# A decoder layer: staircase rows and ScalarE's high maxima in self-attention; sums of four heads and weighings once a pair in cross-attention

## The chip, the cores and the metric

The kernel runs on one core of a Trainium2 chip. The metric is the device time of one execution in microseconds, and the comparison goes by medians of several runs. Engines are named TensorE (PE), VectorE (DVE), ScalarE (ACT), GpSimd (POOL) and SyncE (SP, which only issues transfers here). PEld is TensorE's loading of weights.

## The reference

One layer of a pre-norm decoder on `x` (4 x 512 tokens, width 512), cut to what matters:

```
x = x + attn(layernorm(x))             # 32 query heads of 16, 8 key/value groups, causal, softmax
x = x + xattn(layernorm(x), ctx, ctx)  # per batch 8 heads of 64 rows, softmax over ctx's 512 columns
x = x + ffn(layernorm(x))              # ternary weights, 8-bit activations, gate and up 512->2048, down

def attn(x):   scores = q k^T / 4, masked where key > query; softmax(scores) v, then Wo
def xattn(q, k, v):                    # the tensors are split in heads along their rows (tokens)
    qk = einsum('bdm,bdn->bmn', qh, kh) / 8
    return einsum('bmn,bcn->bcm', softmax(qk, -1), vh)
```

## The kernel before

Each engine has its own program; semaphores tie them together. Three stretches follow each other.

**Self-attention.** `project_qkv` normalises and projects, with queries and keys split in three bf16 parts that are stacked in rows (`STACK` = 96 rows of `qs` and `ks`). There is one step for each pair of batch and group, 32 in all, software-pipelined: in step i TensorE computes the *first scores* of group i (`first_scores`, units F(0) to F(9), queries on the partitions), of which VectorE takes the maxima (`keep_maxima`, L148) with the causal mask `mask_qk` added; the maxima are transposed (`turn_maxima`, L137) and split in a high and a low bf16 row (`split_maxima`, L162 and L164), which `load_maxima` puts in rows 96 and 97 of `qs`. Two steps later the *second scores* S(0) to S(10) (keys on the partitions) contract 98 rows, so that the maximum is already subtracted (L852). The four of them that hold a diagonal block, S(0), S(5), S(8) and S(10), get a second matmul that adds the causal mask: `identb` against `mask_kq`, 4 heads x 128 columns (L855). ScalarE takes the exponential (L787), and `weigh` multiplies by the values in four 32-column tiles side by side (L870). ScalarE copies the result (L797), TensorE turns it (L836, slot `OUT`), VectorE divides (L806, L809). First scores, `OUT` and `TURN` share four banks in the order 0, 1, OUT, 2, TURN, 3 ... 9: a unit may start when the one four places earlier has been read. TensorE's order in a step is F0 S0 F1 S1 turn_outputs F2 S2 turn_maxima F3 S3 F4 S4, the weighings, then F5 S5 ... F9 S9 S10. SyncE and GpSimd load and quantise the feed-forward weights beside it.

**Output projection and cross-attention.** `rest_of_layer` projects, adds and normalises (`attend_output`), then runs `attend_context(i)`, one step for each head; two heads make a pair p. In step i TensorE runs the first scores of head i-1 (L1605, four matmuls over three banks; a matmul waits until the maximum three uses back has been taken) and the second scores of head i-4 (`second_scores`, L1633): four blocks, each the sum of four terms, of which the last subtracts the maxima from `mrows`. The terms run two blocks at a time. `weigh(p, 0)` and `weigh(p, 1)` follow in the odd step 2p+5, `weigh(p, 2)` and `weigh(p, 3)` in the even step 2p+6, all into the bank `pn` (L1646). VectorE takes four maxima a step (L1416), and in even steps the second total (L1446), the low keys (L1428) and the transposed maxima (L1422, `mt`), in odd steps the product with the inverse sums (L1465, `y_done`). GpSimd adds the probabilities (L1175, L1180) and adds the product to the tokens (L1184). ScalarE takes four exponentials a step (L1277), keeps weighted values (`keep_weighted`, L1256) and sums (`keep_sums`, L1305), and rounds keys (`keys`, L1246).

The way of the softmax sums: `sum_probs(p)` (L1661, in step 2p+8) multiplies the totals of the pair's two heads with ones, into two halves of a bank; ScalarE copies it (`den`), its queue moves two rows of it into `few` (step 2p+9), VectorE inverts (L1453, step 2p+10), SyncE writes the result to memory (step 2p+11, L1097) and spreads it over 64 rows for each head (step 2p+12, L1105, one buffer `rden`, behind a wait for the product of the pair before), VectorE multiplies (step 2p+13).

SyncE's program of an odd step begins with `load_maxima`: it waits for `mt_done` and issues four transfers `mrows` <- `mt` (L1044), which the last term of the first second scores in the next, even step waits for. Context rows, low queries and values follow. The queue is in order.

**Feed-forward.** `feed(i)` for 16 tiles of tokens; the last eight steps of `attend_context` run beside its first bodies.

Of the kernel before, what the change touches and what calls it, by code (L numbers as in the profile page):

```python
# [13 lines left out]
P = 128  # L14
# [61 lines left out]
class Steps:  # L76
# [9 lines left out]
    RING, RAW = 5, 6  # L86

# [66 lines left out]
def split_maxima(nc, dve, st, keep, i):  # L154
# [4 lines left out]
    dve.wait_ge(keep["p1_full"], st.use[i, st.TURN] + 1)  # L159
    if due(32 * (j // st.RING)):  # L160
        dve.wait_ge(keep["m_in"][j % st.RING], 32 * (j // st.RING))
    nc.vector.tensor_scalar(mrow[:, j % st.RING, 0, :], maxima, -1.0, None, ALU.mult).then_inc(keep["m_high"], 1)  # L162
# [33 lines left out]
def place_attention(nc, ctx, keep, st):  # L196
# [20 lines left out]
    over("vts", [P, SEQ], at["wg"] + 43 * KB)  # L217
    W = DIM + 2 * P
# [51 lines left out]
def project_qkv(nc, ctx, io, scr, keep, st):  # L270
# [39 lines left out]
    wo_high, padded = m.sem("wo_high"), m.sem("padded")  # L310
# [14 lines left out]
    def sync(sp):  # L325
# [10 lines left out]
        def load_x(b):  # L336
            sp.wait_ge(normed, TPB * b)
            sp.dma_start(x[:], x_d[b]).then_inc(x_in, 16)

# [11 lines left out]
        for b in range(BATCH):  # L351
# [17 lines left out]
            if b == 1:  # L369
                load_stacks(sp, st, scr, keep, 1)  # L370
            elif b == 2:
# [7 lines left out]
    def gpsimd(pool):  # L379
# [7 lines left out]
        for name in ("ident", "identb"):  # L387
# [7 lines left out]
                                base=0, pattern=[[0, GSZ], [1, P]], channel_multiplier=-1).then_inc(consts, 1)  # L395
# [29 lines left out]
        nc.gpsimd.memset(keep["ks"][STACK:P, :, :], 1.0).then_inc(padded, 1)  # L425
        pool.wait_ge(padded, 2)
        for b in range(BATCH):
# [10 lines left out]
    def scalar(act):  # L438
# [43 lines left out]
        for b in range(BATCH):  # L482
# [5 lines left out]
            high_part(b, 2)  # L488
            if more:
                high(b + 1, 0)  # L490
                high(b + 1, 1)
# [9 lines left out]
    def vector(dve):  # L501
# [33 lines left out]
        def early(b, idx):  # L535
            for i, k in early_after(b, idx):
                if k == st.TURN:
                    split_maxima(nc, dve, st, keep, i)
# [155 lines left out]
def self_attention(nc, ctx, io, scr, keep, st):  # L694
# [45 lines left out]
    def gpsimd(pool):  # L740
# [30 lines left out]
        pool.wait_ge(keep["last_out"], 16)  # L771
        pool.wait_ge(keep["scaled"], 3)
# [3 lines left out]
    def scalar(act):  # L776
        for i in range(LAST):
# [13 lines left out]
            for n in range(5):  # L791
                exponential(n)
            if 0 <= j3 < STEPS:
# [7 lines left out]
    def vector(dve):  # L801
# [11 lines left out]
        for i in range(st.EARLY_STEPS, LAST):  # L813
            for k in st.order:
# [4 lines left out]
                elif k == TURN:  # L819
                    split_maxima(nc, dve, st, keep, i)  # L820
# [3 lines left out]
    def tensor(pe):  # L824
        pe.wait_ge(keep["lo_done"], TILES)
        pe.wait_ge(keep["scaled"], 1)
        pe.wait_ge(keep["padded"], 2)
        for i in range(st.EARLY_STEPS, LAST):
# [10 lines left out]
            def second_scores(n):  # L839
# [51 lines left out]
def rest_of_layer(nc, io, scr, keep, out):  # L891
# [5 lines left out]
    PAIRS = HEADS_X // 2  # L897
# [947 lines left out]
```

## Time and profile before

| | |
|---|---|
| median of 3 runs | 792.17 us (792.15 to 793.11) |
| the profiled execution | 791.34 us, its span 789.5 us |
| TensorE busy | 758.5 us, 96% of the span |
| VectorE busy | 637.8 us, 81% |
| ScalarE busy | 491.1 us, 62% |
| GpSimd busy | 423.1 us, 54% |
| self-attention steps | about 93 to 373 us |
| output projection | about 373 to 435 us |
| cross-attention steps | about 435 to 597 us |
| feed-forward | to the end |

Matmuls overlap in the profile: one of 512 columns lasts 0.38 us and the next starts 0.22 us after it, so starts are read, not durations. A matmul in fp32 is recorded as two. Busy time says little of who waits; the bracket at the end of a timeline row does: the engine's idle time ahead of the row and who ended it. The granted clock is 1.00 (2.4 GHz) nearly everywhere.

### The profile page before, as it was taken

To read this page: it belongs to the slowest core of one execution; us is meant where nothing else is said; L and a number is where in the kernel's file an instruction comes from. 1 tells how busy PE (TensorE), PEld (TensorE's weight loads), DVE (VectorE), ACT (ScalarE), POOL (GpSimd) and SP (SyncE) were. 2 spreads that over 40 slices of the span, in tenths; PEclk is the share of its full clock that TensorE was granted. 3 is DMA by queue.
4 is the path that set the end of the run, shared out by engine and by line. 5 is a ranking of instruction groups with operands and counts; after the bars stand their busy time and mean duration, and the time that the engine had idled before them with its cause. 6 is when DMAs were issued, how large, how long until landed. Compare 5 with 4: busy or idle time off the path is not lost.

```text
span 789.5 us, 15365 instructions
## 1 busy us (share of the span) xinstructions
PE 758.5 (96%) x4832; PEld 420.6 (53%) x4886; DVE 637.8 (81%) x1905; ACT 491.1 (62%) x844; POOL 423.1 (54%) x459
## 2 busy tenths in 40 slices
PE   8999999999999999998999899999998999999998
PEld 6777544444444444443777555555543455455543
DVE  7676888889888889881589878888977899888883
ACT  4665567667766776676355555555556576567564
POOL 5554489999999700000234367777886444423331
PEclk9999999999999999999899999999999999999999
DMA  8898674444544311200486434444420011000001
GB/s 289 301 385 282 210 186 136 122 132 133 139 128 130 96 54 52 61 18 3 146 284 236 162 108 136 134 136 135 121 70 18 11 42 41 28 15 27 28 26 42
DMA packets 65888, 94.79 MB, mean 120 GB/s; under 512 B 27184, under 2 KB 38576, under 8 KB 64272
## 3 DMA queue, kind: packets, MB, share of 16 engines
q1 hardware_dynamic: 61344, 80.77, 32.5%
q0 software_dynamic: 3952, 12.98, 5.8%
q8 instruction: 39, 0.64, 0.3%
q14 instruction: 41, 0.34, 0.1%
q10 hardware_dynamic: 512, 0.07, 0.1%
HBM read 72.88 MB, written 20.51 MB: 118 GB/s over the span
## 4 chain that ended last, share of the span: by engine, by line
PE 40%; DVE 5%; issue 3%; ACT 2%; POOL 1%; SPq 0%; DMA 0%; ACTq 0%; DVEq 0%; POOLq 0%
PE r_p L1698 12%; PE r_p L1633 7%; PE r_pn L1646 7%; PE r_p L1728 3%; PE r_pn L1728 3%; PE r_p L1605 3%; PE r_p L1661 2%; PE r_p L1712 2%; DVE r_stats L1384 1%; DVE tok L1403 1%; PE r_p L1587 1%; DVE r_xl L1397 1%; ACT r_xn L1235 1%; DVE r_mx L1416 0%; DVE r_h L1500 0%
## 5 line engine op out<-in xcount | busy, mean ns | idle before, releaser
L787 ACT ACTIVATE b_probs<-ab_j 128x512 f32<-128x512 f32 (+1 forms) x352 | 176.7, 560 | 25.5 <-PE ab_j L852 14.6
L148 DVE CUSTOM_DVE_ANT_0 b_junk<-ab_t,mask_qk 128x128 bf16<-128x128 f32 (+2 forms) x243 | 108.7, 485 | 27.0 <-PE ab_t L128 26.7
L852 PE MATMUL ab_j<-qs,ks 98*128 98x512 bf16 (+1 forms) x352 | 121.8, 361 | 2.9 <-DMA qs<-mrow 1.1
L1277 ACT ACTIVATE r_probs<-r_p 128x512 f32<-128x512 f32 x128 | 69.5, 599 | 65.2 <-PE r_p L1633 63.8
L148 DVE CUSTOM_DVE_ANT_0 b_junk<-ab_e,mask_qk 128x256 bf16<-128x256 f32 (+2 forms) x237 | 103.6, 482 | 0.3 <-issue 0.2
L1416 DVE TENSOR_REDUCE r_mx<-r_p 128x1 f32<-128x512 f32 x128 | 82.4, 675 | 22.1 <-PE r_p L1605 21.2
L1175 POOL TENSOR_TENSOR r_halves<-r_probs 128x1024 f32<-128x1024 f32 x32 | 76.6, 2395 | 34.8 <-DVE r_total L1446 24.9
L1327 ACT ACTIVATE r_silu<-r_p,r_cg 128x512 f32<-128x512 f32 x64 | 44.2, 691 | 53.0 <-PE r_p L1698 51.7
L870 PE MATMUL ab_pv<-b_probs,v 128*32 128x512 f32 (+3 forms) x1024 | 75.6, 436 | 0.0
L1202 POOL TENSOR_SCALAR r_h<-r_h,r_fh 128x1024 f32<-128x1024 f32 x32 | 38.0, 1199 | 64.8 <-DVE r_fh L1546 64.8
L128 PE MATMUL ab_e<-ks,qs 96*128 96x128 bf16 (+3 forms) x269 | 64.0, 300 | 5.3 <-DVE mx L148 0.7
L1698 PE MATMUL r_p<-wu,r_zt 128*128 128x512 bf16 x251 | 65.4, 379 | 0.3
L1698 PE MATMUL r_p<-wg,r_zt 128*128 128x512 bf16 x245 | 63.5, 379 | 2.1 <-ACT r_zt L1367 1.4
L1646 PE MATMUL r_pn<-r_probs,r_vt 128*64 128x512 f32 x256 | 61.3, 599 | 0.5 <-ACT r_y L1256 0.5
L128 PE MATMUL ab_t<-ks,qs 96*128 96x128 bf16 (+2 forms) x243 | 58.6, 301 | 2.4 <-DVE mx L148 0.2
L1500 DVE TENSOR_TENSOR r_h<-r_p,r_silu 128x512 f32<-128x512 f32 x64 | 44.0, 687 | 18.7 <-PE r_p L1698 10.7
L870 PEld LDWEIGHTS ab_pv<-b_probs,v 128*32 128x32 f32 x1024 | 30.0, 109 | 48.3 <-issue 41.6
L1130 POOL MEMSET r_mrows<- 128x1024 f32 x1 | 1.0, 952 | 101.7 <-POOLq L238 101.7
L797 ACT ACTIVATE b_osb<-ab_pv 128x512 f32<-128x512 f32 x32 | 19.1, 597 | 58.2 <-PE ab_pv L870 58.2
L852 PEld LDWEIGHTS ab_j<-qs,ks 98*128 98x128 bf16 x352 | 34.1, 97 | 26.5 <-ACT b_probs L787 10.4
L1508 DVE TENSOR_REDUCE r_hpart<-r_h 128x1 f32<-128x512 f32 x64 | 43.9, 686 | 2.2
L128 PEld LDWEIGHTS ab_e<-ks,qs 96*128 96x128 bf16 x269 | 22.9, 98 | 39.6 <-DVE mx L148 14.8
(177 smaller groups left out, 1761.3 us busy)
## 6 DMA issues: line engine op xcount, KB each, us to landing
qs<-q_parts SPq DMA_DIRECT2D x32, 192.0 KB, 3.3
q_parts<-a_parts SPq DMA_DIRECT2D x15, 384.0 KB, 6.1
a_wst<-in_w_gate SPq DMA_DIRECT2D x4, 1024.0 KB, 7.7
a_wst<-in_w_up SPq DMA_DIRECT2D x4, 1024.0 KB, 9.9
a_wst<-in_w_down SPq DMA_DIRECT2D x4, 1024.0 KB, 8.3
qs<-q_parts SPq DMA_DIRECT2D x32, 128.0 KB, 3.2
b_wst<-in_w_gate POOLq DMA_DIRECT2D x16, 256.0 KB, 3.8
b_wst<-in_w_up POOLq DMA_DIRECT2D x16, 256.0 KB, 3.3
```

The source lines that it names most:

```text
L128: last = nc.tensor.matmul(st.bank(keep, i, k)[:, c:c + w], keep["qs"][0:STACK, s, j, qt * P:(qt + 1) * P], keep["ks"][0:STACK, s, 0:w], st ...
L148: best = nc.vector.tensor_tensor_reduce(out=junk[:, 2 * (st.use[i, k] % slots) + n, 0:w], in0=bank[:, c:c + w], in1=keep["mask_qk"][:, SEQ ...
L787: nc.scalar.activation(pblock(j % 2, kb)[:, j0:j0 + nj, c:c + w], p2[(NE * j + n) % BANKS2][:, 0:nj * w].rearrange("p (j c) -> p j c", j=n ...
L852: last = nc.tensor.matmul(bank, ks[0:STACK + 2, s, kb * P:(kb + 1) * P], qs[0:STACK + 2, s, j0:j0 + nj, kb * P + c:kb * P + c + w], start= ...
L870: last = nc.tensor.matmul(pv[2 * HDIM * j:2 * HDIM * (j + 1), kb * P:], v, pblock(j3 % 2, kb)[:, j, :], start=kb == 0, stop=kb == TPB - 1, ...
L1175: nc.gpsimd.tensor_tensor(halves[:], probs[:, slot, 0:2, :], probs[:, slot, 2:4, :], ALU.add).then_inc(halved, 1)
L1277: nc.scalar.activation(probs[:, 2 * (p % 2) + a, blk, :], p2_bank("s", j, n)[:], ACT.Exp, scale=SCALE).then_inc(p2_used, 1)
L1416: nc.vector.reduce_max(mx[:, p % 2, KD * a + blk:KD * a + blk + 1], p1_bank("f", i, n)[:], AX.X).then_inc(p1_used, 1)
L1633: last = nc.tensor.matmul(p2_bank("s", j, 2 * b + a)[:], weights, right[rows, :], start=term == 0, stop=term == 3)
L1646: last = nc.tensor.matmul(pn[a * H:(a + 1) * H, :], vt[:, 2 * (p % 2) + a, nb, :], probs[:, 2 * (p % 2) + a, nb, :], start=nb == 0, stop=n ...
L1698: last = nc.tensor.matmul(bank[g % len(bank)][:], zt[:, j % 2, k, :], keep[w][:, k, n * 512:(n + 1) * 512], start=k == 0, stop=k == KD - 1)
L1728: last = nc.tensor.matmul(pf[j % 2][:], ht[j % 2][:, k, :], keep["wd"][:, k, :], start=k == 0, stop=k == KF - 1)
```

## The change

In self-attention:

- The causal mask of the diagonal blocks is put partly into the stacks. Rows 98 to 127 (30 = `STAIRS`) of `ks` get -1e30 where row and key agree, and those rows of `qs` are one for the queries from 97 up to the one before that row. The diagonal second scores contract 128 rows instead of 98, and the mask matmul covers 97 (`FLAT`) of a head's 128 columns. GpSimd makes the pattern (two fills, three selections), and SyncE copies it to all slots (`load_stairs`, 30 rows x 100 copies of 256 bytes) behind the stacks of step 1.
- The high maxima are taken by ScalarE (`maxima_high`), after its third exponential of the step, and VectorE, which takes the low ones, waits for that.

In cross-attention:

- `sum_probs` sums four heads at once, in four 32-column tiles, every second even step (10, 14, ...). The copy, the move into `few`, the inverse and the transfers are once for four heads too; the inverse and its way to memory are in steps 13 + 4q, SyncE's spreading in steps 14 + 4q (two buffers `rden`, each behind a wait for the product that last read it).
- The product and the addition to the tokens move from step 2p+13 to 2p+17, with six buffers `y` and eight for the totals.
- The four `weigh` of a pair all run in the even step 2p+6.
- `attend_context` has four more steps, beside feed-forward bodies.

The diff, cut to what sets order and waits:

```diff
+    STAIRS = P - STACK - 2
+    FLAT = P - STAIRS - 1
...
+def maxima_high(nc, act, st, keep, i):
+
+    j = i - 1
+    act.wait_ge(keep["p1_full"], st.use[i, st.TURN] + 1)
+    if due(32 * (j // st.RING)):
+        act.wait_ge(keep["m_in"][j % st.RING], 32 * (j // st.RING))
+    nc.scalar.activation(keep["mrow"][:, j % st.RING, 0, :], st.bank(keep, i, st.TURN)[0:st.BLOCKS, 0:P], ACT.Copy,
+                         scale=-1.0).then_inc(keep["m_high"], 1)
...
+        def load_stairs():
+
+            sp.wait_ge(stairs_done, 3)
+            rows = slice(P - st.STAIRS, P)
+            for part, name, copies in ((0, "ks", st.RING * TPB), (1, "qs", st.RING * GSZ * TPB)):
...
             for n in range(5):
                 exponential(n)
+                if n == 2 and i >= st.EARLY_STEPS and (i, TURN) in st.use:
+                    maxima_high(nc, act, st, keep, i)
...
-                last = nc.tensor.matmul(bank, ks[0:STACK + 2, s, kb * P:(kb + 1) * P],
-                                        qs[0:STACK + 2, s, j0:j0 + nj, kb * P + c:kb * P + c + w], start=True, stop=c > 0)
+                rows = slice(0, P) if c == 0 else slice(0, STACK + 2)
+                last = nc.tensor.matmul(bank, ks[rows, s, kb * P:(kb + 1) * P],
+                                        qs[rows, s, j0:j0 + nj, kb * P + c:kb * P + c + w], start=True, stop=c > 0)
                 if c == 0:
-                    last = nc.tensor.matmul(bank, keep["identb"][:], keep["mask_kq"][:].rearrange("p j c -> p (j c)"), start=False, stop=True)
+                    last = nc.tensor.matmul(bank.rearrange("p (j c) -> p j c", j=GSZ)[:, :, 0:st.FLAT], keep["identb"][:], keep["mask_kq"][:],
+                                            start=False, stop=True)
...
-                p = pair_due(i, 11)
-                if p is not None:
-                    sp.wait_ge(inv_done, p + 1)
...
-                p = pair_due(i, 12)
-                if p is not None:
-                    sp.wait_ge(inv_out, 16 * (p + 1))
-                    if due(p):
-                        sp.wait_ge(y_done, p)
...
+                q = quad_due(i, 13)
+                if q is not None:
+                    sp.wait_ge(inv_done, q + 1)
...
+                q = quad_due(i, 14)
+                if q is not None:
+                    sp.wait_ge(inv_out, 16 * (q + 1))
+                    for p in (2 * q, 2 * q + 1):
+                        if due(p - 1):
+                            sp.wait_ge(y_done, p - 1)
+                        for a in range(2):
+                            at = RUNS * (2 * p + a)
+                            sp.dma_start(rden[a * H:(a + 1) * H, p % 2, :], scr["inv"][at:at + RUNS, :].rearrange("r c -> (r c)")
+                                         .unsqueeze(0).broadcast_to([H, DIM])).then_inc(rden_in[p % 2], 16)
...
-                p = pair_due(i, 13)
+                p = pair_due(i, 17)
                 if p is not None:
-                    dve.wait_ge(rden_in, 32 * (p + 1))
+                    dve.wait_ge(rden_in[p % 2], 32 * (p // 2 + 1))
                     dve.wait_ge(y_kept, p + 1)
...
-                p = pair_due(i, 8)
-                if p is not None and p < LATE_SUMS:
-                    sum_probs(p)
-                p = pair_due(i, 5)
-                if p is not None:
-                    weigh(p, 0)
-                    weigh(p, 1)
+                q = quad_due(i, 10)
+                if q is not None and q < QUADS - 1:
+                    sum_probs(q)
                 p = pair_due(i, 6)
                 if p is not None:
-                    weigh(p, 2)
-                    weigh(p, 3)
-                if i == 2 * LATE_SUMS + 8:
-                    sum_probs(LATE_SUMS)
+                    for nb in range(KD):
+                        weigh(p, nb)
```

## Rows read from the trace of the kernel before

**Rows 1.** Timeline, VectorE, one self-attention step: start, us, engine, line, operation, [idle before]

```profile
203.21 0.29 DVE L148 CUSTOM_DVE_ANT_0 b_junk<-ab_t,mask_qk 128x128 bf16<-128x128 f32 x1 [0.93 <-PE ab_t L128]
...
208.10 0.42 DVE L809 TENSOR_TENSOR tok<-ab_t,b_rec 128x256 f32<-128x256 f32 x1
...
209.13 0.27 DVE L162 TENSOR_SCALAR mrow<-ab_e 16x128 bf16<-16x128 f32 x1
...
211.94 0.29 DVE L148 CUSTOM_DVE_ANT_0 b_junk<-ab_t,mask_qk 128x128 bf16<-128x128 f32 x1 [0.93 <-PE ab_t L128]
```

**Rows 2.** Timeline, TensorE, the same step

```profile
204.61 0.38 PE L855 MATMUL ab_j<-mask_kq,identb 128*128 128x512 bf16 x1
...
204.83 0.38 PE L128 MATMUL ab_t<-ks,qs 96*128 96x512 bf16 x1
...
208.59 0.39 PE L128 MATMUL ab_t<-ks,qs 96*128 96x512 bf16 x1
...
209.07 2.36 PE L870 MATMUL ab_pv<-b_probs,v 128*32 128x512 f32 x32
...
211.36 0.39 PE L128 MATMUL ab_t<-ks,qs 96*128 96x128 bf16 x2
```

**Rows 3.** Timeline, ScalarE, the same step

```profile
208.55 1.12 ACT L787 ACTIVATE b_probs<-ab_j 128x384 f32<-128x384 f32 x2 [0.29 <-PE ab_j L852]
```

**Rows 4.** Timelines; window table (from:to, length, engines busy, PEclk, DMA share, GB/s)

```profile
19.20 0.24 POOL L401 TENSOR_SCALAR a_veps<-a_mv 128x4 f32<-128x4 f32 x1 [2.14 <-DVE a_mv L511]
...
64.00:65.00 1.00, 1.00 (x6) 0.75 (x4) 1.00 (x3) 0.00 (x0) 0.96 (x1) 1.00 0.09 32
...
85.33 1.65 DVE L586 TENSOR_SCALAR wo_hi<-a_wraw 128x2048 fp32r<-128x2048 f32 x1 [1.52 <-DMA a_wraw<-in_wo]
```

**Rows 5.** Window table, cross-attention steps 17 to 32

```profile
500.38:579.79 79.41, 79.12 (x482) 42.47 (x480) 68.81 (x109) 45.55 (x87) 62.80 (x37) 1.00 0.44 125
```

**Rows 6.** Timeline, TensorE, cross-attention: end of step 12, step 13

```profile
477.93 1.08 PE L1661 MATMUL r_p<-r_total,ones 128*64 128x512 f32 x4
...
478.83 1.89 PE L1646 MATMUL r_pn<-r_probs,r_vt 128*64 128x512 f32 x8
...
480.65 0.49 PE L1605 MATMUL r_p<-r_kh,r_qh 64*128 64x512 f32 x2
...
481.91 0.52 PE L1605 MATMUL r_p<-r_kh,r_qh 64*128 64x512 f32 x2
...
483.29 1.94 PE L1646 MATMUL r_pn<-r_probs,r_vt 128*64 128x512 f32 x8
...
485.15 0.50 PE L1605 MATMUL r_p<-r_kh,r_qh 64*128 64x512 f32 x2
```

**Rows 7.** Timeline, VectorE, the same steps

```profile
477.65 0.53 DVE L1453 RECIPROCAL r_inv<-r_few 16x64 f32<-16x64 f32 x1
...
481.18 2.49 DVE L1416 TENSOR_REDUCE r_mx<-r_p 128x1 f32<-128x512 f32 x4
...
483.58 0.78 DVE L1465 TENSOR_TENSOR r_y<-r_y,r_rden 128x512 f32<-128x512 f32 x1
```

**Rows 8.** Timeline, ScalarE, the same steps

```profile
482.60 0.59 ACT L1256 ACTIVATE r_y<-r_pn 128x512 f32<-128x512 f32 x1
```

**Rows 9.** Timelines: SyncE in steps 12 and 13; the first maxima and their matmul

```profile
479.06 1.14 SPq L1105 DMA_DIRECT2D r_rden<-inverse_sums  x2
...
481.07 2.21 SPq L1044 DMA_DIRECT2D r_mrows<-r_mt  x4
...
435.69 2.35 SPq L1044 DMA_DIRECT2D r_mrows<-r_mt  x4
...
439.08 0.78 PE L1633 MATMUL r_p<-r_mrows,r_unit 64*128 64x512 f32 x2 [0.40 <-DMA r_mrows<-r_mt]
```

**Rows 10.** Timeline, TensorE; window table behind its idle time

```profile
436.29 0.49 PE L1605 MATMUL r_p<-r_kh,r_qh 64*128 64x512 f32 x1 [2.06 <-DVE r_mx L1416]
...
437.00:446.00 9.00, 8.56 (x46) 6.01 (x48) 8.01 (x14) 6.32 (x11) 0.18 (x2) 0.81 0.57 183
```

More of the change, by code:

```diff
@@ L488, in scalar @@
             high_part(b, 2)
+            if (1, st.TURN) in early_after(b, 2):
+                maxima_high(nc, act, st, keep, 1)
             if more:
@@ L1011, in p2_bank @@
         def p2_bank(*key):
-            return p2[SBANKS - 1] if key[0] == "sum" and key[1] >= LATE_SUMS else p2[p2_use[key] % SBANKS]
+            return p2[SBANKS - 1] if key == ("sum", QUADS - 1) else p2[p2_use[key] % SBANKS]
         def pair_due(i, behind):
@@ L1017, in pair_due, with quad_due @@
             return s // 2 if s >= 0 and s % 2 == 0 and s < HEADS_X else None
+        def quad_due(i, behind):
+            s = i - behind
+            return s // 4 if s >= 0 and s % 4 == 0 and s < HEADS_X else None
         @block.sync
@@ L1282, in attend_context @@
                     keep_weighted(p)
-                p = pair_due(i, 9)
-                if p is not None:
-                    act.wait_ge(p2_used, p2_use["sum", p] + 1)
-                    if due(p - 1):
-                        act.wait_ge(inv_done, p - 1)
-                    for a in range(2):
-                        act.dma_start(few[a * RUNS:(a + 1) * RUNS, p % 2, :],
-                                      den[a * H:a * H + 1, :].rearrange("o (r c) -> o r c", r=RUNS)).then_inc(few_in, 16)
+                q = quad_due(i, 11)
+                if q is not None:
+                    act.wait_ge(p2_used, p2_use["sum", q] + 1)
+                    if due(q - 1):
+                        act.wait_ge(inv_done, q - 1)
+                    act.dma_start(few[:, q % 2, :], den[0:3 * PART + 1:PART, :].rearrange("a (r c) -> a r c", r=RUNS)).then_inc(few_in, 16)
                 exponential(1)
@@ L1649, in weigh, with sum_probs @@
                     last.then_inc(weighted, 1)
-            def sum_probs(p):
-                pe.wait_ge(first_total, p + 1)
-                pe.wait_ge(second_total, p + 1)
-                if p < LATE_SUMS:
-                    pe.wait_ge(p2_used, p2_use["sum", p] - SBANKS + 1)
-                elif p == LATE_SUMS:
+            def sum_probs(q):
+                pe.wait_ge(first_total, 2 * q + 2)
+                pe.wait_ge(second_total, 2 * q + 2)
+                if q < QUADS - 1:
+                    pe.wait_ge(p2_used, p2_use["sum", q] - SBANKS + 1)
+                else:
                     pe.wait_ge(p2_used, P2_USES)
-                else:
-                    pe.wait_ge(p2_used, p2_use["sum", p - 1] + 1)
-                for a in range(2):
-                    last = nc.tensor.matmul(p2_bank("sum", p)[a * H:(a + 1) * H, :], keep["ones64"][:], total[:, 2 * (p % 2) + a, :], start=True, stop=True)
+                for a in range(4):
+                    last = nc.tensor.matmul(p2_bank("sum", q)[a * PART:(a + 1) * PART, :], keep["ones64"][:, 0:PART], total[:, (4 * q + a) % TSLOTS, :],
+                                            start=True, stop=True)
                 last.then_inc(summed, 1)
```

131 lines of the change are left out of this document (72 added, 59 removed).

## The prediction

> **What bounds the kernel now.** I read three views in this order: the busy table by windows, to see in which stretch TensorE leaves time; then the timelines of TensorE and VectorE side by side through one self-attention step and through one pair of cross-attention steps; last SyncE's issues in that pair, because the change moves waits on that queue. The reader should see two different limits.
>
> In self-attention TensorE looks busy almost throughout, but it does not set the pace. VectorE starts a step's first reduction after the weighing at 203.21 and again at 211.94: a step of 8.73 us [rows 1]. In between it runs without a pause until `tok` is written at 208.52 (208.10 + 0.42). Only then is the bank of `OUT` free for unit 4: TensorE starts it at 208.59, and from there go unit 4, S(4), the weighings (`x32`, from 209.07), unit 5 at 211.36, and VectorE's 211.94 [rows 1, 2]. This loop sets the step: 5.31 us of VectorE, then 3.35 us of TensorE in which no mask matmul lies, plus 0.07 us between.
>
> In cross-attention TensorE is the limit: eight pairs of steps (17 to 32) take 79.41 us with 79.12 us busy [rows 5]. An odd step lasts 4.50 us (480.65 to 485.15): scores until the weighing starts at +2.64, then 1.86 us for half of the weighings. An even step adds the sum, 0.90 us (477.93 to 478.83) [rows 6]. I count times below from the start of an odd step, "+".
>
> **Self-attention: nothing.** The mask matmul takes 0.22 us from start to start (204.61 to 204.83) for 512 columns; 388 columns save 0.053 us, and 128 of them 6.8 us [rows 2]. All four of a step (S(0), S(5), S(8), S(10)) lie between unit 5 and unit 3 of the next step, beside VectorE's unbroken 5.31 us. With that cover they are worth 0; without it -6.8, which I keep as the bound. The staircase rows widen a contraction from 98 to 128 rows and add no column; the mask matmul itself already contracts 128 rows at 0.22 us, so 0. VectorE gives up the high maxima, 0.27 us, at 209.13, in the part of the step that ends in 0.93 us of waiting [rows 1]: 0, while it waits longer. ScalarE takes them after its third exponential, where it has 0.29 us idle and the next exponential starts at 208.55 [rows 3]; the shortest thing near it is VectorE's 0.27, the longest its own 0.60 us for 512 columns [rows 8]. Either ends before VectorE asks at 209.13, so the new wait of VectorE (behind it are the low maxima and unit 3) costs 0. GpSimd's five new operations lie in its 2.14 us of idle time ahead of 19.20 us; the fill there is paid. The two staircase transfers (3,000 pieces, 0.77 MB) enter SyncE's queue behind the stacks of step 1, some microseconds ahead of the stretch 64 to 65 us. In that stretch the DMA engines have 91% of their time free, so most of that queue is worked off; what is left could delay `wo`, on which VectorE already waited 1.52 us at 85.33 [rows 4]. I count 0.4 us for that and 0.3 us gained because VectorE, which is the limit just before the steady steps, has one operation less: 0, between -7 and +1.5.
>
> **Cross-attention, work of TensorE.** A sum of four costs what a sum of two did if the four 32-column tiles run together. The self-attention weighing does that: 32 matmuls of 320 columns on average in 2.29 us (209.07 to 211.36) [rows 2], against 8 of 512 columns in 1.86 us for 64-column tiles [rows 6], twice the rate. So 0.90 us per quad; one after another it would be 1.8. The weighings of a pair are together 3.72 us, and an odd step without them runs into the next with +2.41 (two halves of 1.26, 480.65 to 481.91, less the 0.11 for the change of tile shape that the first half holds and the second does not). TensorE alone would then need 2.41 + 2.64 + 3.72 = 8.77 us a pair and 0.45 for its half of a sum, 9.2 instead of 9.9.
>
> **What stops it: the queues beside it.** With three score banks, the last first-score matmul of a step waits for the first maximum of the same step. In an odd step VectorE runs four maxima from +0.53 to +3.02 and then the product, 2.93 to 3.71 [rows 7]. The next step's first maximum ends some 0.65 later, and the matmul can start at +4.36 instead of +3.67: before, the weighing of the odd step covered that. Before step 17 there is no product; then ScalarE decides, which keeps the weighted values at +1.95 (0.59 us) and so ends its second exponential at about +3.05 [rows 8]; the four terms that wait for its bank take 0.95, and that matmul starts at +4.05. After it come 1.38 us of scores and 3.72 of weighings. The reciprocal, now in odd steps, puts 0.5 us (0.53 long [rows 7]) ahead of the product in every second pair, and that pair is also the one with the sum: 4.36 + 0.5 + 1.38 + 0.90 + 3.72 = 10.86 us.
>
> The other pairs have a worse wait. SyncE issues in order. At step 14 + 4q it now spreads the inverse sums of pairs 2q and 2q + 1, and for the second it waits for `y_done` of product 2q - 1. That product (`pair_due(i, 17)` on VectorE) runs in step 15 + 4q, the step after. Queued behind the wait is everything SyncE issues for that step: first the four transfers of the maxima (`load_maxima`) which S(0) of step 16 + 4q needs for its last term. Today they are issued right behind VectorE's transpose, at 481.07, +0.42. With the change SyncE wakes at +3.71 and issues two broadcasts, 1.14 us, to +4.85. The time from the first of the four issues to the matmul that waited for it is seen once: 435.69 to 439.08, 3.39 us [rows 9]. So this matmul starts at about +8.3 instead of +3.8: TensorE stands 4.5 us. The pair then takes 8.27 + 0.23 + 1.38 + 3.72 = 13.6 us. Four pairs have it: q = 1 to 4, steps 19, 23, 27, 31 (for q = 0 there is no wait, for q = 5 no maxima are left). The context rows behind it, needed by ScalarE's `keys` in the same even step, land at about +10.1; the low keys and the transpose end near +13, before the next step: no more.
>
> The clock comes on top. After TensorE's idle 2.06 us before 436.29 the stretch 437 to 446 shows a granted clock of 0.81, that is 3.4 us at 1.2 instead of 2.4 GHz, costing 1.7 us of matmul time [rows 10]. Here it stands twice as long; I take 1.7 for each of the four, bounds 0 and 3.4. The Trainium skill, "TensorE: Matmul & The Clock Gate", section "HAM oscillation — how this bites in real kernels", says that a loop which waits for a transfer between groups of matmuls falls to half clock every time and pays anew; the trace has one case, which agrees. By that rule the time is the one below, without it 6.8 us less, the second rival.
>
> **The sum.** Pairs of steps 17 to 32: 4 x (10.86 + 13.6 + 1.7) = 104.6, against 79.4: +25.2. Pairs of steps 5 to 16: 8.8 (steps 5, 6), three of 4.05 + 1.38 + 3.72 = 9.15 and two of 10.1 with the sum make 56.4, against 9.0 + 5 x 9.9 = 58.5: -2.1. Steps 33 to 36 lose about 0.9 to ScalarE (no weighing beside the exponentials), and the feed-forward part starts one sum, 0.9, earlier: 0. The later products (two more beside the feed-forward steps) lie on VectorE where it is not the limit. Together +23. The profiled execution took 791.34 us (span 789.5), 0.8 below the median 792.17; 791.3 + 23.1 = 814.4, on the median's scale 815.
>
> **Rivals.** First, TensorE's work decides everywhere: mask -6.8, early pairs 54.4 against 58.5 (-4.1), late pairs 8 x 9.22 = 73.8 against 79.4 (-5.6), so -16.5: 776, faster. For it speaks the full TensorE row; against it the 0.93 us of VectorE's loop and the order of the wait on `y_done`, which is in the diff. It decides if VectorE's chain were shorter than TensorE's 2.41 us step. Chance 0.08. Second, the stalls without the clock: +16.3, 808.5; the single case speaks against it, but it lay beside other short gaps. 0.17. Third, the wait of SyncE is harmless (maxima early enough): 4 x (10.86 + 9.46) = 81.3, +1.9 - 2.1, 792, within 0.2%; it needs a slack of a whole step that I don't see. 0.06. Fourth, four-column sums one after another or a second period at half clock: +6 to +7 on the forecast, 821. 0.09. The forecast itself: 0.60, own range 810 to 819.
>
> **Numbers.** 815 us. Leaving out the first and third rival and some of the spread: 802 to 823. Faster by over 0.2% (about what a measurement of this kernel can tell) 0.08, within 0.2% 0.05, slower 0.87.
>
> **What would show it.** Four gaps of 4 to 5 us on TensorE between third and fourth term of S(0), released by the `r_mrows` transfer; SyncE waiting for L1465's product at those four places; granted clock 0.5 behind them; other pairs at about 10.9 us; self-attention steps still 8.73 us, with shorter mask matmuls and longer waits for VectorE. A step of 8.5 us there, or no gap at steps 20, 24, 28 and 32, would make the prediction wrong.

## The result, and the profile after

The changed kernel takes 816.58 us (median of four runs, 814.09 to 819.54); the kernel before takes 792.16 us beside it. The ratio is 1.032, with a 95% interval of 1.030 to 1.035: slower, as forecast (815, range 802 to 823). The profiled execution took 814.09 us with a span of 812.4; that of before took 791.34 with 789.5. So 22.9 us of span are to be found.

First the page of the changed kernel: busy time by engine, then the group of the last score term (L1681 is what L1633 was: busy us, mean ns, idle us just before it and its releaser).

```profile
PE 758.9 (93%) x4886; PEld 420.2 (52%) x4886; DVE 632.4 (78%) x1865; ACT 487.4 (60%) x868; POOL 423.5 (52%) x464
...
L1681 PE MATMUL r_p<-r_mrows,r_unit 64*128 64x512 f32 x128 | 34.4, 435 | 18.0 <-DMA r_mrows<-r_mt 18.0
```

TensorE is busy for the same 758.9 us as before (758.5), although it has less to do (part of the work now runs at half clock, as shown below), and it stands 18.0 us waiting for the maxima's transfer. The kernel before stood 0.4 us there. The timeline of TensorE through the first long pair, steps 19 and 20 (start, us, engine, line, operation, idle before):

```profile
499.65 0.50 PE L1653 MATMUL r_p<-r_kh,r_qh 64*128 64x512 f32 x1 [0.30 <-DVE r_mx L1464]
...
501.02 1.06 PE L1707 MATMUL r_p<-r_total,ones 128*32 128x512 f32 x8
502.02 3.65 PE L1694 MATMUL r_pn<-r_probs,r_vt 128*64 128x512 f32 x16
505.60 0.50 PE L1653 MATMUL r_p<-r_kh,r_qh 64*128 64x512 f32 x2
...
509.03 0.62 PE L1681 MATMUL r_p<-r_ql,r_kh 64*128 64x512 f32 x2
513.95 0.80 PE L1681 MATMUL r_p<-r_mrows,r_unit 64*128 64x512 f32 x2 [4.30 <-DMA r_mrows<-r_mt]
514.54 0.63 PE L1653 MATMUL r_p<-r_kh,r_qh 64*128 64x512 f32 x2
...
516.81 5.29 PE L1694 MATMUL r_pn<-r_probs,r_vt 128*64 128x512 f32 x16
522.02 0.50 PE L1653 MATMUL r_p<-r_kh,r_qh 64*128 64x512 f32 x2
```

The odd step 19 starts at 505.60. The fourth term of S(0) of step 20 starts at 513.95, at +8.35, after 4.30 us of standing. Behind it the same matmuls take longer: the sixteen weighings 5.29 us instead of 3.65. The pair lasts 16.42 us. The same stretch by windows (from:to, length, busy of PE, PEld, DVE, ACT, POOL, then the granted clock, DMA share, GB/s):

```profile
512.00:513.00 1.00, 0.00 (x0) 0.00 (x0) 0.00 (x0) 0.00 (x0) 1.00 (x1) 1.00 0.09 32
513.00:514.00 1.00, 0.05 (x2) 0.06 (x2) 0.00 (x0) 0.00 (x0) 0.92 (x2) 0.66 0.01 2
514.00:516.00 2.00, 2.00 (x10) 1.62 (x12) 0.80 (x2) 1.14 (x3) 1.92 (x2) 0.50 0.89 293
...
520.00:521.00 1.00, 1.00 (x6) 0.28 (x4) 0.00 (x0) 0.00 (x0) 0.00 (x0) 0.93 0.01 1
```

The granted clock falls to 0.50 while TensorE still stands and is back at 1.00 at about 520.1: some 6.8 us at 1.2 GHz. Between 512 and 513 GpSimd alone works. What SyncE does in that time (its issues), and the product that it waits for:

```profile
501.47 9.12 SPq L1154 DMA_DIRECT2D r_rden<-inverse_sums  x4
510.69 2.22 SPq L1092 DMA_DIRECT2D r_mrows<-r_mt  x4
```
```profile
504.60 0.21 DVE L1470 STREAM_TRANSPOSE r_mt<-r_mx 128x32 f32<-128x32 f32 x1
506.14 2.48 DVE L1464 TENSOR_REDUCE r_mx<-r_p 128x1 f32<-128x512 f32 x4 [1.33 <-PE r_p L1653]
508.54 0.68 DVE L1513 TENSOR_TENSOR r_y<-r_y,r_rden 128x512 f32<-128x512 f32 x1
```

VectorE has turned the maxima at 504.8. SyncE issues their transfers at 510.69, because of the four broadcasts ahead of them: the first two are issued from 501.47, the other two wait for the product, which ends at 509.22. The transfers of the maxima, which [rows 9] show at +0.42 of the odd step, are now at +5.09.

The starts of the odd steps, read off TensorE's timelines of the kernels (the first L1653 behind the weighings; with split weighings two steps make a pair), give the length of each pair. All tables below are built so:

| pairs, us | steps 7 to 16 | steps 17 to 32 |
|---|---|---|
| before | 9.85, 9.86, 9.85, 9.86, 9.87 | 9.83 to 9.87, one of 10.5 |
| after | 8.93, 9.93, 9.13, 9.98, 8.93 | 10.61, 16.42, 10.60, 16.71, 10.59, 16.70, 10.60, 14.98 |

Steps 7 to 16 give 2.4 us back, steps 17 to 32 cost 107.2 instead of 79.4 us. The rest of the span, from the start to step 7, is 3.0 us shorter, and between step 33 and the feed-forward part 0.55 us are lost; together +22.9 (-3.0 - 2.4 + 27.8 + 0.5). The self-attention steps are 8.73 us as before.

### The profile page after: what moved, and what is told of

It is laid out like the page before. It is cut to its first block, busy times and chain, and to the rows that moved or that the text cites. A ratio compares the mean times of both kernels' runs of the same rounds, so it can differ in the third digit from the quotient of the medians.

```text
span 812.4 us, 15336 instructions
## 1 busy us (share of the span) xinstructions
PE 758.9 (93%) x4886; PEld 420.2 (52%) x4886; DVE 632.4 (78%) x1865; ACT 487.4 (60%) x868; POOL 423.5 (52%) x464
## 4 chain that ended last, share of the span: by engine, by line
PE 36%; DVE 8%; issue 3%; ACT 2%; SPq 2%; POOL 1%; DMA 1%; DVEq 0%; POOLq 0%; ACTq 0%
PE r_p L1739 12%; PE r_pn L1694 8%; PE r_p L1681 5%; PE r_p L1769 3%; PE r_pn L1769 3%; DVE r_mx L1464 3%; PE r_p L1753 2%; PE r_p L1653 2%; DVE r_stats L1432 1%; PE r_p L1707 1%; SPq L1092 1%; DVE tok L1451 1%; DMA r_mrows<-r_mt 1%; DVE r_xl L1445 1%; SPq L1154 1%
## 5 line engine op out<-in xcount | busy, mean ns | idle before, releaser
L824 ACT ACTIVATE b_probs<-ab_j 128x512 f32<-128x512 f32 (+1 forms) x352 | 172.7, 560 | 24.1 <-PE ab_j L893 15.2
L893 PE MATMUL ab_j<-qs,ks 128*128 128x512 bf16 (+2 forms) x352 | 121.9, 361 | 2.6 <-DMA qs<-mrow 1.4
L1739 PE MATMUL r_p<-wg,r_zt 128*128 128x512 bf16 x256 | 65.7, 379 | 1.4 <-ACT r_zt L1415 1.4
L1694 PE MATMUL r_pn<-r_probs,r_vt 128*64 128x512 f32 x256 | 63.4, 640 | 0.0
L1681 PE MATMUL r_p<-r_mrows,r_unit 64*128 64x512 f32 x128 | 34.4, 435 | 18.0 <-DMA r_mrows<-r_mt 18.0
L893 PEld LDWEIGHTS ab_j<-qs,ks 98*128 98x128 bf16 (+1 forms) x352 | 34.2, 97 | 23.2 <-ACT b_probs L824 12.2
```

The source lines that it names most:

```text
L824: nc.scalar.activation(pblock(j % 2, kb)[:, j0:j0 + nj, c:c + w], p2[(NE * j + n) % BANKS2][:, 0:nj * w].rearrange("p (j c) -> p j c", j=n ...
L893: last = nc.tensor.matmul(bank, ks[rows, s, kb * P:(kb + 1) * P], qs[rows, s, j0:j0 + nj, kb * P + c:kb * P + c + w], start=True, stop=c > 0)
L1681: last = nc.tensor.matmul(p2_bank("s", j, 2 * b + a)[:], weights, right[rows, :], start=term == 0, stop=term == 3)
L1694: last = nc.tensor.matmul(pn[a * H:(a + 1) * H, :], vt[:, 2 * (p % 2) + a, nb, :], probs[:, 2 * (p % 2) + a, nb, :], start=nb == 0, stop=n ...
L1739: last = nc.tensor.matmul(bank[g % len(bank)][:], zt[:, j % 2, k, :], keep[w][:, k, n * 512:(n + 1) * 512], start=k == 0, stop=k == KD - 1)
```

## The experiments

Each kernel was timed beside the kernel before on the same chip, and the ratio is to that. The median of before was 789.1 to 791.4 on those chips.

### The wait on SyncE

**spread_late.** The spreading of the second pair is moved to where its product is already done.

```diff
-                    for p in (2 * q, 2 * q + 1):
-                        if due(p - 1):
-                            sp.wait_ge(y_done, p - 1)
...
+                    spread(2 * q)
+                q = quad_due(i, 16)
+                if q is not None:
+                    spread(2 * q + 1)
```

> The changed kernel with one thing moved: SyncE spreads the inverse sums of pair 2q + 1 in step 16 + 4q instead of 14 + 4q, when the product that it waits for is already done. My theory: the four standstills of 4.5 us and the half clock behind them all vanish, and the gaps of TensorE ahead of the last term of S(0) in steps 20, 24, 28 and 32 with them. The four pairs take about 10 us instead of 16.4, 16.4, 16.7 and 15: 64.5 - 40 = 24.5 less than the changed kernel, so 792. Rival 1 (the transfer of the maxima itself, or its queue, is late whatever SyncE waits for): the gaps stay, 812 or more. Rival 2 (the half clock does not come from the standstill but from the longer chains of the odd steps): the gaps vanish, 0.5 of granted clock stays, about 805.

Measured: 791.39 us, ratio 1.001 (0.999 to 1.003). The waits for the maxima are gone and the clock is 1.00 in steps 17 to 32. SyncE's issues in the same place now:

```profile
503.47 1.14 SPq L1159 DMA_DIRECT2D r_rden<-inverse_sums  x2
506.64 2.23 SPq L1092 DMA_DIRECT2D r_mrows<-r_mt  x4
```

The pairs of steps 17 to 32 begin 10.59, 9.22, 10.60, 9.21: the pair that took 16.4 takes 9.22. The later four are 11.07, 10.12, 10.61 and some 9.2 us, with no wait of TensorE over 0.9 us. Both rivals fall; the one moved wait carries the whole loss. What is left of the change is worth nothing in sum.

**filled.** The wait stays, and TensorE gets something to do in it.

```diff
+                again = 6 if b == 0 and j in (16, 20, 24, 28) else 0
+                for at, (term, (left, right)) in enumerate(terms[0:3] * again + terms):
```

> The changed kernel with the first three terms of the first score group computed seven times instead of once in steps 20, 24, 28 and 32, where TensorE otherwise stands 4.5 us: 18 more pairs of matmuls of 0.23 us, 4.2 us, the last set is the one that counts. SyncE's wait stays. Theory (a pair with a stall costs 4.5 us of standing and about 3 us of half clock that the standing brings): the pairs of 16.4 to 16.7 us become about 13.7, granted clock 1.00 in them, and the median is some 10 us below the changed kernel's, 805 to 807. Rival 1 (the half clock has another cause): pairs and time as in the changed kernel, 814 to 819. Rival 2 (the transfer waits for something of TensorE's): the gap moves behind the fill and the time rises.

Measured: 805.25 us, ratio 1.020 (1.017 to 1.023). Windows over the first and the last of the four pairs with the wait, of the changed kernel and then of this one:

```profile
505.60:522.02 16.42, 12.09 (x58) 6.14 (x56) 9.13 (x12) 5.25 (x10) 9.21 (x5) 0.79 0.27 82
...
587.22:602.20 14.98, 10.43 (x58) 5.76 (x56) 10.68 (x16) 4.72 (x9) 9.97 (x6) 0.89 0.19 55
```
```profile
510.95:524.72 13.77, 13.29 (x96) 8.39 (x94) 9.50 (x12) 5.18 (x10) 9.34 (x5) 1.00 0.32 97
...
583.02:596.30 13.28, 12.67 (x92) 8.37 (x92) 9.38 (x13) 4.72 (x9) 9.35 (x5) 1.00 0.25 61
```

With matmuls in place of the standing the clock stays at 1.00. The four pairs take 53.55 us instead of 64.81: the half clock costs 11.3 us, 2.8 a pair. Against the 9.22 us of a pair without the wait the remaining 13.4 leave 4.2 for the wait itself. So of the 7.0 us that a wait costs, 4.2 are the queue and 2.8 the clock.

The 2.8 is a mean of unequal parts. In the changed kernel the fourth wait is as long as the others (4.50 us), but its low clock ends sooner:

```profile
595.00:596.00 1.00, 0.23 (x2) 0.23 (x4) 0.00 (x0) 0.00 (x0) 0.92 (x2) 0.62 0.05 5
...
598.00:599.00 1.00, 1.00 (x6) 0.20 (x4) 1.00 (x1) 0.27 (x1) 1.00 (x1) 0.68 0.04 9
```

That is 3.4 us at 1.2 GHz instead of 6.8, and the pair is 1.70 us longer than its filled counterpart (14.98 against 13.28), where the other three are 2.65 to 3.46 us longer. What decides between 3.4 and 6.8 no run shows.

### The order of the product and of the weighings

Both on top of spread_late.

**product_even.** The product goes back to even steps, one step later; the spreading follows it.

```diff
-                p = pair_due(i, 17)
+                p = pair_due(i, 18)
```

> The kernel of the late spreading, with the product and its addition moved back to the even steps (one step later than in the changed kernel), and the spreading with it. My theory: in the changed order the product delays the next step's first maximum, so odd steps without a weighing run into a stop ahead of their fourth score group; with the product in even steps the pairs with and without the sum lose about 0.3 to 0.6 us each over eight pairs: 3 us less than the late spreading, 789. Rival (ScalarE's exponentials limit there anyway, as in the early pairs): no difference, within 1 us.

Measured: 788.66 us, ratio 0.999 (0.997 to 1.002), 2.7 below spread_late, whose interval it overlaps. In the profiled executions the pairs are shorter: 10.00, 8.95, 9.99, 9.02 instead of 10.59, 9.22, 10.60, 9.21, and steps 17 to 30 take 68.0 instead of 71.4 us. As a whole that execution is not faster (790.93 against 790.09), because its first copy of weighted values in self-attention comes 4.6 us later, at 111.6 instead of 107.1 (the start of the kernel is treated below). So the gain is seen in the steps of one execution each and not shown in the time.

**weigh_split.** The sixteen weighings of a pair are split over two steps as before.

```diff
+                p = pair_due(i, 5)
+                if p is not None:
+                    weigh(p, 0)
+                    weigh(p, 1)
                 p = pair_due(i, 6)
                 if p is not None:
-                    for nb in range(KD):
-                        weigh(p, nb)
+                    weigh(p, 2)
+                    weigh(p, 3)
```

> The kernel of the late spreading, with the weighings of a pair in two groups in two steps as before, so that the change keeps the sum of four, the product in odd steps and the self-attention part. My theory: the half of the weighings in the odd step covers the wait for the bank of scores again and TensorE is busy throughout; the sum of four, 1.0 us per four heads instead of 0.9 per two, leaves a pair at about 9.45 instead of 9.9 us: 14 pairs, 6 us below the kernel before, 786. Rival (four-column sums save nothing, since the sum itself takes longer than two did or a wait takes its place): 791 to 792.

Measured: 787.33 us, ratio 0.997 (0.995 to 1.000). Pairs alternate between 10.58 and 8.99 us, 9.78 on average and not the 9.45 I worked out. The long one holds an odd step of 5.09 us (500.60 to 505.69) where others take 4.50. VectorE ahead of its maxima, and TensorE's row in that step:

```profile
499.05 1.96 DVE L1481 TENSOR_TENSOR r_kl<-r_k,r_kh 128x512 fp32r<-128x512 f32 x1
500.93 0.68 DVE L1469 TENSOR_REDUCE r_mx<-r_p 128x1 f32<-128x512 f32 x1
501.64 0.21 DVE L1475 STREAM_TRANSPOSE r_mt<-r_mx 128x32 f32<-128x32 f32 x1
501.78 1.25 DVE L1469 TENSOR_REDUCE r_mx<-r_p 128x1 f32<-128x512 f32 x2
```
```profile
502.48 0.50 PE L1658 MATMUL r_p<-r_kh,r_qh 64*128 64x512 f32 x1 [0.20 <-DVE r_mx L1469]
```

The low keys, 1.96 us, lie in the even step ahead. That step has no sum now in every second pair and is 1.0 us shorter, so the last maximum of it is reduced only at 500.93, 0.33 us into the odd step, and the odd step's first ends at 502.4, after TensorE has asked for its bank: the weighings begin 1.94 us after the third first score (501.88 to 503.82) where the next step has 1.34 (506.97 to 508.31). In the pair with the sum the same maximum starts 0.67 us ahead of the odd step (510.51 to 511.18) and nothing waits. The kernel before needs 19.7 us for two pairs, this one 19.57: a sum of four saves 0.7 us in the even steps, and the 0.59 of the odd step gives most of it back.

**split_even.** Both together, with the wide staircase pieces of a later section.

> All that the earlier runs point to, without the looser order in self-attention: late spreading, product in even steps, weighings split over two steps, staircase of wide pieces. With the product in even steps alone the pairs took 10.0 and 8.95 us; with the split alone 10.58 and 8.99, where the reciprocal and the product in one odd step cost 0.6. Theory: both together give 10.0 and 8.95 with a last sum started earlier (1.7 us less ahead of the feed-forward part), and the head as in the kernel before: some 6 us below it, 783.5 to 785. Rival (the split's gain and the even product's are the same gain): as the product in even steps with a good head, 786.

Measured: 797.72 us, ratio 1.009 (1.007 to 1.011). The expectation missed, on the far side of both theories, and the reason that it gives for the 0.6 us (reciprocal and product in one step) is not what the rows above show. From step 17 on, most steps come out at 5.07, 4.50, 6.06 and 5.49 us where weigh_split has 4.51, 4.49, 5.09 and 5.49. VectorE and TensorE at such a place:

```profile
519.30 0.93 DVE L1518 TENSOR_TENSOR r_y<-r_y,r_rden 128x512 f32<-128x512 f32 x1
520.15 1.28 DVE L1469 TENSOR_REDUCE r_mx<-r_p 128x1 f32<-128x512 f32 x2
```
```profile
520.88 0.50 PE L1658 MATMUL r_p<-r_kh,r_qh 64*128 64x512 f32 x1 [1.09 <-DVE r_mx L1469]
```

The product stands behind the transposition, ahead of the odd step's maxima, and pushes them by 0.85 us, on top of the late low keys. With whole weighings TensorE spends 3.6 us in front of that step and VectorE catches up; with the weighings split it has 1.9 us, and TensorE waits 1.09. The place of the product was tried in both places of the weighings, but split_even also has the wide staircase pieces, which lie ahead of these steps. In these rows the place of the product is good or bad only together with the place of the weighings.

### Self-attention

**self_only.** The kernel before with the self-attention part of the change alone.

```diff
+                rows = slice(0, P) if c == 0 else slice(0, STACK + 2)
-                    last = nc.tensor.matmul(bank, keep["identb"][:], keep["mask_kq"][:].rearrange("p j c -> p (j c)"), start=False, stop=True)
+                    last = nc.tensor.matmul(bank.rearrange("p (j c) -> p j c", j=GSZ)[:, :, 0:st.FLAT], keep["identb"][:], keep["mask_kq"][:],
+                                            start=False, stop=True)
```

> The kernel before with the self-attention part of the change alone: staircase rows, mask matmuls of 388 instead of 512 columns, high maxima on ScalarE. My theory: VectorE's loop sets the step, so it stays 8.73 us and the time stays within 1 us of before (791 to 793), with more idle time of TensorE ahead of unit 4 or longer waits. Rival (TensorE's time counts): 128 masks less 0.053 us each, steps of about 8.5 us, 785.5.

Measured: 794.38 us over twelve runs, ratio 1.003 (1.001 to 1.006): the steps are 8.73 us, as the theory has it, but the ratio puts the kernel 2.5 us above before (0.4 to 4.5), which it hasn't. The steps first. VectorE's and TensorE's rows of the changed kernel that answer to [rows 1, 2]:

```profile
212.01 0.29 DVE L150 CUSTOM_DVE_ANT_0 b_junk<-ab_t,mask_qk 128x128 bf16<-128x128 f32 x1 [1.25 <-PE ab_t L130]
```
```profile
208.02 0.39 PE L130 MATMUL ab_e<-ks,qs 96*128 96x128 bf16 x2 [0.25 <-DVE mx L150]
```

VectorE waits 1.25 us at the end of its loop instead of 0.93, which is the high maxima that it gave up; TensorE waits 0.25 us ahead of a unit where the timeline of before shows no wait (207.96), which fits the masks' saving of four times 0.053 us. The step stays.

**two_masks.** The mask of one unit a step issued twice, on the kernel before.

```diff
+                for turn in range(0 if c else 2 if n == 5 else 1):
```

> The kernel before with the mask matmul of one of the four masked units of each self-attention step (S(5)) issued twice: 32 matmuls of 0.22 us more, 7.0 us of TensorE's work. Theory (all masks lie beside VectorE's unbroken 5.31 us, so TensorE's time there counts for nothing as long as its slack of some 0.4 us a step lasts): steps stay 8.73 us, time within 1 us. Rival (TensorE's work counts in the step): steps of 8.95 us, 7 us more.

Measured: 794.90 us, ratio 1.005 (1.003 to 1.007), steps of 8.90 us. Neither theory had 0.17. The rows say why:

```profile
215.17 0.29 DVE L148 CUSTOM_DVE_ANT_0 b_junk<-ab_t,mask_qk 128x128 bf16<-128x128 f32 x1 [0.93 <-PE ab_t L128]
...
215.87 0.08 DVE L148 DVE_READ_ACCUMULATOR2_ANT mx<- 128x1 f32 x1
216.04 0.69 DVE L148 CUSTOM_DVE_ANT_0 b_junk<-ab_e,mask_qk 128x512 bf16<-128x512 f32 x1
```

VectorE's third reduction follows the first at +0.87 where the kernel before has +0.70 (203.21 to 203.91): S(5)'s mask lies ahead of the unit that this reduction needs, TensorE was only 0.05 us ahead of VectorE there (the reduction starts 0.57 us behind its matmul when it waits for it, at 215.47 and 216.04, and 0.62 us behind it in before, at 212.03 and 212.65), and 0.22 - 0.05 = 0.17 reach the step. So the loop stands, but it is tight: a mask taken away gives nothing, a mask added at this place costs three quarters of its time.

**loop_before, loop_self.** The looser order of a step, on the kernel before and on self_only. ScalarE copies the weighted values two exponentials later.

```diff
-            W(0); W(1); W(2); W(3)
-            F(5); S(5); F(6); S(6); F(7); S(7); F(8); S(8); F(9); S(9); S(10)
+            W(0)
+            F(5); S(5); W(1); F(6); S(6); W(2); W(3); F(7); S(7); F(8); S(8); F(9); S(9); S(10)
```

> The kernel before with the order of a self-attention step loosened: one of the four weighing groups stays ahead of unit 5, one follows S(5), two follow S(6), and ScalarE copies the weighted values two exponentials later. Masks are as before, 512 columns. Theory (the step is a loop of 5.31 us VectorE and 3.35 us TensorE, of which 2.29 us are weighings): the loop loses most of the weighings, and TensorE's own work, about 8.3 us, sets the step: 32 steps less 0.4 each, 778 to 780. Rival (TensorE's work sets the step of 8.73 already): no gain, 791.

> The same looser order on the kernel with the self-attention part of the change: masks of 388 columns, high maxima on ScalarE. Theory (the mask's 6.8 us were worth nothing only because VectorE's loop hid them): with TensorE at its limit they now count, 4 times 0.053 us a step, about 0.2 us a step and 6 us in all below the looser order on the kernel before, apart from what the staircase transfers cost ahead of the first step. Rival (the staircase saves nothing on TensorE): within 1 us of it, or above.

Measured: 797.43 us, ratio 1.010 (1.007 to 1.012), and 798.91 us, ratio 1.011 (1.008 to 1.013). Steps are 9.00 and 8.95 us. Both theories missed; only the rival for the second kernel, nothing gained on the first, is near. TensorE in one such step:

```profile
204.85 1.06 PE L872 MATMUL ab_pv<-b_probs,v 128*32 128x512 f32 x8
...
206.61 0.85 PE L872 MATMUL ab_pv<-b_probs,v 128*32 128x384 f32 x8
...
207.93 0.86 PE L872 MATMUL ab_pv<-b_probs,v 128*32 128x256 f32 x16
```

The weighings take 1.00 + 0.79 + 0.79 = 2.58 us in three places (start to start of what follows) instead of 2.29 in one, and VectorE waits 0.49 and 0.63 us for units behind them. TensorE is busy 8.78 us of the 9.00; it was 8.48 of 8.73. My 8.3 us for TensorE's own work was wrong: apart from gaps of 0.25 us it needed the step already. So TensorE's work fills the new step to within 0.22 us; how much of that rest is VectorE's was not measured. In the looser order the shorter masks are worth 0.05 us a step, not 0.2. Whether a looser order of another shape would let them count stays open.

### The start of the kernel

In the profiled run of self_only the copies of the weighted values begin at 112.2 us instead of 106.4. VectorE's row for `wo`, and SyncE's issues behind the staircase:

```profile
90.31 1.23 DVE L622 TENSOR_SCALAR wo_hi<-a_wraw 128x2048 fp32r<-128x2048 f32 x1 [4.67 <-DMA a_wraw<-in_wo]
```
```profile
58.12 1.06 SPq L355 DMA_DIRECT2D ks<-a_stairs  x1
59.24 0.90 SPq L355 DMA_DIRECT2D qs<-a_stairs  x1
60.25 6.28 SPq L364 DMA_DIRECT2D q_parts<-a_parts  x1
```

The wait for `wo` is 4.67 us instead of 1.52 [rows 4], and the issue right behind the staircase takes 6.28 us. In the window 90 to 100 us the granted clock is 0.66.

**stairs_early.** The same two transfers behind the stacks of step 0.

```diff
             if b == 0:
                 load_stacks(sp, st, scr, keep, 0)
+                load_stairs()
```

> The kernel with the self-attention part alone, with its two staircase transfers issued on SyncE behind the stacks of step 0 instead of step 1, some 22 us earlier. In the profiled run of the self-attention part alone the store behind the staircase transfers took 6.3 us to be issued and the load of wo was late: VectorE waited 4.7 us for it, and the first context copy of self-attention came at 112.2 instead of 106.4. Theory (the 3,000 small pieces of the staircase hold the queue, and wo behind them): here the wait for wo is back at about 1.5 us, the first context copy at about 106.5, and the median 3 us lower, at 790 to 791. Rival (the head of the kernel varies by itself, the staircase has no part): no difference to the self-attention part alone.

Measured: 790.12 us, ratio 1.001 (0.999 to 1.002); the wait for `wo` is 2.62 us (1.5 expected), the first copy at 108.4 (106.5 expected).

**wide_stairs.** A source of 512 columns, a quarter of the pieces.

```diff
-    over("stairs", [P, 2, P], at["wg"] + 45 * KB, BF16)
+    over("stairs", [P, 2, SEQ], at["wg"] + 45 * KB, BF16)
```

> The kernel with the self-attention part alone, with a staircase source of 512 instead of 128 columns, so that the two transfers consist of a quarter of the pieces (750 of 1 KB instead of 3,000 of 256 bytes) for the same 0.77 MB, at the same place in SyncE's queue. GpSimd's five operations on it are wider. Theory (the number of small pieces holds the queue ahead of wo): the store behind the staircase is issued in about 1.6 us instead of 6.3, VectorE waits about 1.5 us for wo, and the median is that of the kernel before, within 1 us. Rival (the bytes count, or GpSimd's operations): as the self-attention part alone, 3 to 4 us above the kernel before.

Measured: 791.15 us, ratio 1.000 (0.999 to 1.002).

```profile
86.75 2.08 DVE L622 TENSOR_SCALAR wo_hi<-a_wraw 128x2048 fp32r<-128x2048 f32 x1 [1.09 <-DMA a_wraw<-in_wo]
```
```profile
61.17 0.56 SPq L364 DMA_DIRECT2D q_parts<-a_parts  x1
61.84 2.98 SPq L364 DMA_DIRECT2D k_parts<-a_parts  x1
```

The issue behind the staircase takes 0.56 us, the one after it 2.98, and `wo` is waited for 1.09 us. Both kernels are level with before where self_only is not, so the small pieces explain its loss best. But the intervals touch (self_only from 1.001, stairs_early up to 1.002), and the wait for `wo` varies by itself. Of the seven profiled kernels with narrow pieces behind step 1, four waited 3.67 to 4.67 us and three 1.12 to 2.42, the changed kernel (1.43) and spread_late (1.12) among the latter although the issue behind the staircase took 6.07 and 5.56 us there. The kernels with wide pieces waited 0.62 to 2.56 us, stairs_early 2.62, and before, loop_before and two_masks, which have no staircase, 1.31 to 2.47. That the small pieces cause the long waits is likely and not shown.

**split_wide.** The best two parts together: weigh_split with wide pieces.

> The kernel with the late spreading, the product in odd steps and the weighings of a pair split over two steps, with the staircase source of 512 columns. With narrow pieces its median was 3.3 us below the kernel before; its cross-attention took 221.0 us where that of the kernel before took 225.4, and its profiled run waited 3.7 us for wo. Theory (the gains of the cross-attention part, 4 us, and the wide pieces' head, which is that of the kernel before, add up): 4 to 5 us below the kernel before, ratio 0.994 to 0.995. Rival (the head comes out as with the narrow pieces): ratio 0.997.

Measured: 789.42 us, ratio 0.999 (0.998 to 1.001); theory and rival both missed. The profiled run, the fastest of the twelve, has what was expected: a wait for `wo` of 0.62 us, pairs of 10.57 and 9.01, 785.62 us. The other eleven runs lie at 787 to 791. No version was found that is measurably faster than the kernel before.

## Why the prediction was right

The forecast of 815 us and its main mechanism hold. By its own steps:

- **Self-attention, 0.** The steps are 8.73 us with shorter masks and without the high maxima on VectorE, and the waits moved where the text said. What it gave too little is the account of how tight the step is. It named VectorE's loop as the limit and put the masks' cover at its unbroken 5.31 us; two_masks shows that TensorE was 0.05 us from being late in it.
- **The staircase transfers, +0.4.** Undersized, if the runs of self_only read right: its ratio of 1.003 is 2.5 us of 790.6, and its profiled run waited 3.2 us longer for `wo`. The prediction looked at free DMA share in 64 to 65 us; it did not look at the queue, where the next issue stood 6.28 us. The same stand, 6.07 us, cost the changed kernel's profiled run nothing, so which step failed here stays open.
- **The sum of four, 0.90.** It takes 1.00 us (501.02 to 502.02). The bound of 1.8 is out.
- **Early pairs, 9.15 and 10.1.** They took 8.93 to 9.13 and 9.93 to 9.98: 46.90 for steps 7 to 16.
- **Late pairs with sum and reciprocal, 10.86.** 10.59 to 10.61. The product does delay the next step's first maximum and TensorE waits 0.30 us there, at +4.66 (499.65 less 494.99) as 4.36 + 0.5 had it at +4.86; 0.2 us too much.
- **The wait of SyncE.** Term 4 of S(0) at +8.35, forecast +8.27; gaps of 4.30, 4.49, 4.55 and 4.50 us, forecast 4.5; four places, steps 20, 24, 28 and 32. spread_late shows it as the cause. The third rival, a harmless wait, is what spread_late makes of the kernel, and its 792 is what that measured: 791.4.
- **The clock, 1.7 a pair.** This is the term that was mis-sized. filled measures 2.8 a pair, 11.3 in all against 6.8. In [rows 10] the clock was low for 3.4 us; here it is low for some 6.8 us behind the first three waits and for 3.4 us behind the fourth, whose cost of 1.70 us is the forecast one. So the price of 3.4 low microseconds was right, and how long the clock stays low was wrong three times in four. I took the one case of the trace and held the double as a bound, and the value lies nearer to that end. The Trainium skill, "TensorE: Matmul & The Clock Gate", section "HAM oscillation — how this bites in real kernels", says that such a wait is followed by half clock every time; the changed kernel shows it four times in four.
- **Steps 33 to 36 and the last sum, 0.** +0.5.

The late pairs were forecast at 104.6 and took 107.2, of which the clock explains +4.5 and the pairs with the sum -1.0. That the sum of 814.4 meets the profiled execution's 814.1 so closely is luck, because a part that the forecast did not have went the other way: 3.0 us came off ahead of step 7, of which 0.35 by the end of self-attention. The rest lies between the last copy of self-attention and the first score terms of cross-attention. That stretch takes 66.1 us in before, 63.7 in the changed kernel, and 63.7 and 65.3 in self_only and stairs_early, which have the same instructions there; it goes with how long the clock is low there (granted clock 0.71 in 370 to 380 us of before, 1.00 in the changed kernel, 0.88 in stairs_early). It is 63.7 us as well in loop_before and two_masks, whose instructions there are those of before. So it is not the change's, and the median of 816.6 is the fairer number to hold against 815.

## What to carry to other kernels

On a queue that issues in order, a semaphore wait is a wait for everything behind it: when an issue is moved earlier, compare the step of its semaphore with the step of each issue that follows. A stand of TensorE can cost more than its length: here 4.2 us of delay brought 2.8 us of half clock with it. Count that, and if the wait can't go, work that is thrown away is worth having in it. Placement of small VectorE work is not additive: two orders that each shortened the steps lengthened them together.

## What the runs showed of the hardware

- Four stands of TensorE of 4.30 to 4.55 us each brought a granted clock of 0.50, which began within the stand and lasted 6.8 us three times and 3.4 us once. In [rows 10] it lasted 3.4 us and began at about 439.1, some 3 us behind the end of the 2.06 us gap, with shorter gaps between. Work in the gap kept 2.4 GHz throughout (granted clock 1.00 in all four pairs).
- Two transfers of 3,000 pieces of 256 bytes were issued in 2 us, and then SyncE's next issue took 6.28 us in self_only and 6.07 in the changed kernel; with 750 pieces of 1 KB (wide_stairs) the next two took 0.56 and 2.98.
- The self-attention weighings on 32-column tiles cost 2.29 us in one row of 32 and 2.58 us in three places of a step, with the score matmuls of another tile shape between them (before, loop_before).
